# Two dense attention layers: blocks of 512 queries instead of 256, and the side that is held still in the value product exchanged

## The reference, cut to what matters

```python
h = maximum(layernorm(x), 0);  x = x + L0(h, adj)        # first block, not touched here
h = maximum(layernorm(x), 0);  x = x + L1(h, adj)        # two layers of this form:
def gat_layer(x, W, adj):                                # x 4096 x 256, adj 4096 x 4096
    Wh, Ws = split(x @ W, 2, axis=-1)
    a = softmax(Wh @ Ws.T, axis=-1) * adj
    return leaky_relu(a @ Wh + x, 0.01)
```

## Time and profile before

| | us |
|---|---|
| median of 3 runs | 2611.19 (2610.53 to 2612.25) |
| the profiled execution | 2612.48, its span from first to last instruction 2610.7 |
| first block | up to 925 |
| projection and attention of g0 | 925 to 981, 981 to 1770 |
| projection and attention of g1 | 1774 to 1817, 1817 to 2605 |

### The profile page before, as it was taken

How to read it: one execution, slowest core, us unless ns; L and a number is a source line. 1 busy time by engine, 2 the same in 40 slices (tenths; PEclk the granted TensorE clock), 3 DMA queues, 4 the chain that set the end, 5 groups by cost and what they waited for, 6 DMA issues and landing times. The chain is left out here.

```text
span 2610.7 us, 47736 instructions
## 1 busy us (share of the span) xinstructions
PE 2480.9 (95%) x18360; PEld 2346.5 (90%) x18360; DVE 2210.9 (85%) x2942; ACT 1694.8 (65%) x2348; POOL 1523.2 (58%) x932
## 2 busy tenths in 40 slices
PE   4699999999999979999999999987999999999997
PEld 2588888888888869999999999987999999999997
DVE  8899999998989646888888888894788888888888
ACT  6899999999999754555555555553555555555554
POOL 3899999999999802444434444350245445444446
PEclk8799999999999989999999999999999999999999
DMA  3332323233323021333333333233133333333333
GB/s 109 107 94 89 94 90 93 91 95 93 95 90 93 13 100 47 96 97 107 94 98 102 98 96 107 90 114 109 58 101 114 102 95 120 95 105 111 102 98 106
DMA packets 100980, 248.21 MB, mean 95 GB/s; under 512 B 9360, under 2 KB 51088, under 8 KB 100752
## 3 DMA queue, kind: packets, MB, share of 16 engines
q1 hardware_dynamic: 98880, 243.30, 30.5%
q10 hardware_dynamic: 1872, 1.84, 0.2%
HBM read 232.52 MB, written 12.58 MB: 94 GB/s over the span
## 5 line engine op out<-in xcount | busy, mean ns | idle before, releaser
L91 PE MATMUL l0b_acc<-l_h_parts,l0b_turned_hi 128*128 128x512 f32 x1984 | 727.2, 406 | 19.3 <-POOL l0b_turned_lo L541 19.2
L541 POOL TENSOR_TENSOR l0b_turned_lo<-l0b_turned,l0b_turned_hi 128x1024 fp32r<-128x1024 f32 x256 | 614.3, 2416 | 45.0 <-ACT l0b_turned_hi L578 43.3
L92 PE MATMUL l0b_acc<-l_h_parts,l0b_turned_lo 128*128 128x256 f32 x1984 | 558.3, 281 | 0.0
L1133 POOL TENSOR_TENSOR g0b_sum_wide<-g0b_sum_wide,g0b_slab 128x512 f32<-128x512 f32 x240 | 311.3, 1297 | 396.1 <-DVE g0b_masked_psum L1241 386.0
L1133 POOL TENSOR_TENSOR g1b_sum_wide<-g1b_sum_wide,g1b_slab 128x512 f32<-128x512 f32 x240 | 315.5, 1315 | 339.5 <-DVE g1b_masked_psum L1241 328.7
L91 PEld LDWEIGHTS l0b_acc<-l_h_parts,l0b_turned_hi 128*128 128x128 f32 x1984 | 376.0, 190 | 112.7 <-POOL l0b_turned_lo L541 29.7
L92 PEld LDWEIGHTS l0b_acc<-l_h_parts,l0b_turned_lo 128*128 128x128 f32 x1984 | 374.2, 189 | 0.8
L578 ACT CAST l0b_turned_hi<-l0b_turned 128x1024 fp32r<-128x1024 f32 x256 | 268.1, 1047 | 67.6 <-PE l0b_acc L92 50.1
L80 PE MATMUL g0b_acc<-g_wh_parts,g0b_part_hi 128*128 128x256 f32 x1024 | 293.6, 287 | 6.8 <-DVE g0b_part_lo L1247 5.7
L80 PE MATMUL g1b_acc<-g_wh_parts,g1b_part_hi 128*128 128x256 f32 x1024 | 293.6, 287 | 5.6 <-DVE g1b_part_lo L1247 4.5
L80 PE MATMUL g0b_score_psum<-g0b_q_block,g_vt_hi 128*128 128x256 f32 x1024 | 290.3, 284 | 2.5 <-DVE g0b_q_block L1277 1.4
(11 more groups left out here) (231 smaller groups left out, 7218.6 us busy)
## 6 DMA issues: line engine op xcount, KB each, us to landing
g_adj_ring<-in_adj_blocks_dram SPq DMA_DIRECT2D x256, 512.0 KB, 3.6
l_adj_ring<-in_adj_quads_dram SPq DMA_DIRECT2D x128, 512.0 KB, 3.5
l0b_x_in<-in_x_dram SPq DMA_DIRECT2D x32, 128.0 KB, 2.4
x_rows<-l0b_x SPq DMA_DIRECT2D x32, 128.0 KB, 2.4
g0a_rows<-x_rows SPq DMA_DIRECT2D x8, 512.0 KB, 5.8
g0b_y<-x_rows SPq DMA_DIRECT2D x16, 256.0 KB, 4.0
v_rows<-g0b_y SPq DMA_DIRECT2D x16, 256.0 KB, 4.5
g1a_rows<-v_rows SPq DMA_DIRECT2D x8, 512.0 KB, 5.8
```

Of the source, the lines that this page charges most:

```text
L91: pe.matmul(out, lhs_hi, rhs, start=first, stop=False)
L92: return pe.matmul(out[:, width:], lhs_lo, rhs[:, :width], start=False, stop=False)
L541: pool.tensor_tensor(turned_lo[:, m % PART_RING, :, :], turned[:, m % TURN_RING, :, :], turned_hi[:, m % PART_RING, :, :].bitcast(F32), AL ...
L1133: pool.tensor_tensor(sum_wide[:], sum_wide[:], half_of(c, e), ALU.add).then_inc(summed, 1)
```

## The change

A block has 512 queries (`BLOCK = BANK`), a chunk has 2 key tiles (`CHUNK = 2`), so a layer has 8 blocks of 16 chunks, and still 128 chunks with 1024 elements per partition each. `score` moves 512 columns of queries. In the value product the 128 columns of Wh are held still and 512 queries of the parts move, so that `acc` holds the output turned, and 12 matmuls make a chunk. `TO_SHIFT`, `TO_SPLIT`, `TO_WEIGH` follow PER and become 17, 18 and 19 steps. At a block's end ACT copies `acc` (`copy_out`), PE turns it back with 8 transposes (`turn_out`), DVE drains from there, ACT does the leak.

The high and low parts of Wh no longer fit: the projection stores them to memory, a quad of 1 MB at a time (`store_wh`), and waits for all of them at its end; the attention fetches 512 KB with every chunk (`fetch_wh`) once PE has done the chunk three before, and the adjacency behind it.

Three banks (`side_psum`) now serve every short-lived result of PE in turn: queries, scores, maximum, sum and the turned-back output. A product waits for whatever used its bank three turns before.

```diff
-    BLOCK = 256
+    BLOCK = BANK
-    CHUNK = 4
+    CHUNK = 2
-    SLOTS = 11
+    SLOTS = PER + 3
-        wh_parts = keep.sbuf("wh_parts", [P, T, 2, D], F32R)
...
+                    def store_wh(c):
+                        sp.wait_ge(out_lo_made, OUTS * (c + 1))
+                        wait(sp, wh_stored, 16 * c)
+                        stage = wh_stage[:, (c % 2) * OUTS:(c % 2 + 1) * OUTS, :, :, :].bitcast(F32)
+                        sp.dma_start(wh_dram[:, c, :], stage.rearrange("p o t h d -> p (o t h d)")
+                                     ).then_inc(wh_stored, 16)
...
+                    sp.wait_ge(wh_stored, 16 * QUADS)
...
                     def out_high(c):
+                        wait(act, wh_stored, 16 * (c - 1))
...
+            COPY_OUT, TURN_OUT, DRAIN = TURN_SUM + 1, TURN_SUM + 2, TURN_SUM + 3
...
+            def turns_of_step(n):
+                b = block_at(n, Q_AT)
+                if b is not None and b + 1 < BLOCKS:
+                    yield from (("query", KT * (b + 1) + m) for m in range(KT))
+                if n < CHUNKS:
+                    yield "score", CHUNK * n
+                b = block_at(n, TURN_OUT)
+                if b is not None:
+                    yield from (("out", 2 * b + k) for k in range(2))
+                for kind, offset in (("max", TURN_MAX), ("sum", TURN_SUM)):
+                    b = block_at(n, offset)
+                    if b is not None:
+                        yield kind, b
+                if n < CHUNKS:
+                    yield "score", CHUNK * n + 1
...
+                    def fetch_wh(c):
+                        wait(sp, products, c - ADJ_SLOTS + 1)
+                        sp.dma_start(wh_ring[:, c % ADJ_SLOTS, :, :, :].rearrange("p t h d -> p (t h d)").bitcast(F32),
+                                     wh_by_chunk[:, c % PER, :]).then_inc(chunk_in[c % ADJ_SLOTS], 16)
...
+                    def copy_out(b):
+                        act.wait_ge(products, PER * (b + 1))
+                        wait(act, out_turned, 2 * b)
+                        act.copy(turned_out[:], acc[:]).then_inc(out_copied, 1)
...
-                        for i in range(SUBS):
-                            cols = slice(i * P, (i + 1) * P)
+                        for d in range(KT):
+                            cols = slice(d * P, (d + 1) * P)
                             last = three_products(
-                                pe, acc[:, i, 0:D], (part_hi[:, c % 2, q, cols], part_lo[:, c % 2, q, cols]),
-                                (wh_parts[:, j, 0, :], wh_parts[:, j, 1, :]), j == 0, j == T - 1)
+                                pe, acc[:, d, :],
+                                (wh_ring[:, c % ADJ_SLOTS, e, 0, cols], wh_ring[:, c % ADJ_SLOTS, e, 1, cols]),
+                                (part_hi[:, c % 2, e, :], part_lo[:, c % 2, e, :]), j == 0, j == T - 1)
```

More of the change, by code:

```diff
@@ L1089, in block_at, with bank, tile_of @@
                 return b if rest == 0 and 0 <= b < BLOCKS else None
+            def turns_of_step(n):
[13 more added lines that the diff above has]
+                    yield "score", CHUNK * n + 1
+            order = [("query", m) for m in range(KT)] + [use for n in range(ENDS) for use in turns_of_step(n)]
+            turn_of = {use: turn for turn, use in enumerate(order)}
+            def bank(kind, k):
+                return side_psum[:, turn_of[kind, k] % BANKS, :]
+            def tile_of(c, e):
+                return slab[:, c % SLOTS, e, :]
             with nc.Block() as block:
@@ L1170, in q_high @@
                     def q_high(b):
-                        act.wait_ge(q_made, b + 1)
-                        wait(act, score_made, HALVES * (b - 1))
-                        act.copy(q_block[:, b % 2, 0, :, :], q_bank(b)).then_inc(q_hi_made, 1)
+                        for m in range(KT):
+                            act.wait_ge(q_made, KT * b + m + 1)
+                            if m == 0:
+                                wait(act, score_made, CHUNK * PER * (b - 1))
+                            act.copy(q_block[:, b % 2, 0, m, :], bank("query", KT * b + m)).then_inc(q_hi_made, 1)
                     def normalise(b):
@@ L1304, in _, with wait_for_bank @@
                             totals(b)
-                        if drained is not None:
-                            leak(drained)
+                        if n < CHUNKS:
+                            join_max(n, 0)
                 @block.tensor
                 def _(pe):
-                    def wait_for_bank(turn):
-                        before = turn - SCORE_BANKS
-                        if before in half_at:
-                            pe.wait_ge(score_taken, half_at[before] + 1)
-                        if before in q_at:
-                            pe.wait_ge(q_lo_made, q_at[before] + 1)
+                    def wait_for_bank(kind, k):
+                        turn = turn_of[kind, k]
+                        if turn < BANKS:
+                            return
+                        last_kind, j = order[turn - BANKS]
+                        if last_kind == "score":
+                            pe.wait_ge(score_taken, j + 1)
+                        elif last_kind == "query":
+                            pe.wait_ge(q_lo_made, j + 1)
+                        elif last_kind == "max":
+                            pe.wait_ge(neg_step, 3 * j + 1)
+                        elif last_kind == "sum":
+                            pe.wait_ge(total_step, 2 * j + 1)
+                        else:
+                            pe.wait_ge(scaled, 2 * (j + 1))
@@ L1366, in turn_sum, with turn_out @@
                                                 ident)
                         last.then_inc(sum_turned, 1)
-                    def weigh(c, q):
+                    def turn_out(b):
+                        pe.wait_ge(out_copied, b + 1)
+                        for k in range(2):
+                            wait_for_bank("out", 2 * b + k)
+                            for i in range(SUBS // 2):
+                                here = slice((k * SUBS // 2 + i) * P, (k * SUBS // 2 + i + 1) * P)
+                                for d in range(KT):
+                                    last = pe.transpose(bank("out", 2 * b + k)[:, i * D + d * P:i * D + (d + 1) * P],
+                                                        turned_out[:, d, here], ident)
+                            last.then_inc(out_turned, 1)
```

296 lines of the change are left out of this document (148 added, 148 removed).

## The result

The kernel after takes **2740.78 us** (median of 4 runs, 2732.89 to 2745.62) beside 2611.7 us before: ratio 1.0492, 95% interval 1.0475 to 1.0509. It is slower, by 129 us where 109 were forecast. Its profiled execution took 2741.81 us, its span 2740.0.

What follows compares the result with a forecast made beforehand. PE was taken to bound the steady attention. Attention +33.1 us a layer, twice +66, projections +33 and ends +10 made +109 us, 2720 us on the median; range 2640 to 2765 us.

Steps and rivals of the forecast that it cites:

- What one product costs: PE's products: one 512 wide takes 235 ns where two 256 wide take 240; each ns is worth 5.9 us.
- The bounds: Limits for one 512-wide product on PE: 227 ns if overhead is paid once per product, 240 if it goes with columns.
- the first rival: PE's products: overhead goes with each product, 227 ns wide, −48 us, giving 2672 us; chance 0.19.
- The steady steps: Attention outside the tail: −14.7 us a layer, step 5.64 us, PE stays the bound, adjacency lands after 5.4 us without delaying PE.
- the forecast's own first two waits: Block end, step 36: PE loses 0.75 us at the output's turning back and 0.75 us at the second score.
- A bank is waited for at each block's end: Shared banks at six block ends: PE loses 4.7 us each, 3.2 of it behind DVE's drain; +28.2 us a layer.
- The clock "at full": Sign of being right: PE halts of about 3 us, six a layer, leave the granted clock at full.
- The third rival: Step 37's halt lowers the clock, 2.4 us more for each of 12, or a transfer is late: 2749 us; chance 0.16 together with 240 ns pace.
- A longer tail: Attention's tail: value products lag 19 steps, not 11; a fetch loop makes it 80 us, 75 without; net +11.9 us.
- Between the phases, and the ends: Projections +33 us from storing Wh at 5.2 us a store; last outputs and g1's residual sum, ends +10 us.
- the signs that the forecast listed as wrong: Pace under 217 ns, stores under 4 us, no PE wait on the drain, or PE waiting every step for the parts.
- steps 36 and 37: Steps at a block's end where bank order was followed: PE loses 0.75 and 0.75 us, then 3.2 us.

Runs made afterwards that it cites:

- the pace measurement: Separate kernel computing none of the reference: sequences of 97 products, wide, narrow and alternating, alone or beside other engines; 226.6 ns wide, 120 ns narrow.
- the first edit: The kernel after with a block's drain one step earlier on DVE, behind that step's last maximum; 2669.34 us, ratio to before 1.0218.
- the cure: The kernel after with the adjacency fetched two chunks ahead, once VectorE frees its slot, on its own semaphores; 2668.6 us, ratio to before 1.0219.
- the last kernel: Earlier drain, early adjacency, overlapping stores, staging tile kept into attention, and first three adjacency fetches moved behind the barrier; 2587.06 us, ratio to before 0.9906.
- the kernel with both cures: The kernel after with the drain one step earlier and the adjacency fetched two chunks ahead; 2611.78 us, ratio to before 0.9999.
- each half: The kernel after with only the drain one step earlier (2669.34 us), or only the adjacency fetched two chunks ahead (2668.6 us).

## Why the prediction was right, and where it was not

The time, 2741, lies in the range and 21 us over the forecast. But one of the forecast's steps was 49 us too dear, and two others, the late transfers (some 30 us beyond what it had) and the clock (some 20), were together about as much too cheap.

- **What one product costs.** This term was mis-sized: 235 ns taken, 226.7 measured. 8.3 ns x 5880 products are 49 us that the kernel got back. The bounds held the value, and the reason for the lower one (the 13.3 ns are paid once a product) is what the pace measurement showed. The doubt written beside it ("its neighbours are narrow ones") was the cause, and the first rival, 227 ns, had this term right.
- **The steady steps.** "A landing up to 3 us later still costs nothing" failed. The landing was sized well (5.25 for 5.4), but the argument followed only the parts to PE's value products. ScalarE's high part stands ahead of its copies of the scores, and those free PE's banks; the forecast saw this at a block's end and took it for nothing in the steps of the queries and the maximum. By the two kernels: 653.1 us with halts and the adjacency ahead, 678.6 with it late, so 25.5 us in g0 and 24.3 in g1. 1.65 us at each of the six block ends are the forecast's own first two waits (it had 1.5); the other 15 or so a layer it had at nothing. In g0 those are 7.6 us of idle time in the steps named and 8.4 us of longer busy time, 5 of them by more half clock (27.3 for 17.1 us); the last 3 stay open, and so does where g1, with 17.1 us of half clock in both kernels, has its 5.
- **A bank is waited for at each block's end.** Right: 3.20 us, six a layer, released by VectorE's drain, and 4.85 us a block end for 4.7.
- **The clock "at full"** failed. It was forecast from a fall 4.1 us after the end of work, and 3.20 us of idle time brought it down in ten of twelve cases. The third rival had the mechanism at 29 us; 44.4 us at half clock are 22, and the first edit gave back 20.5.
- **A longer tail.** The loop over the fetch is there, and the cure gives the 75 us that the forecast named without it, nearly (79.2 and 76.3). Its size was low: 84.9 and 91.1 for 80, 16 us in all. In g1's tail the clock fell as well, mean 0.90.
- **Between the phases, and the ends.** Right in mechanism and size: +28.0 for +33, and +8.6 for +10. The restart at half clock came, 10.2 us at 1.2 GHz in each layer; where it didn't (the last kernel), g0's stage up to the first weighing was 2.5 us shorter than in after.

So for the stretch from first weighing to last score of g0: 624.6 us if nothing waits (the kernel with both cures). By the forecast's terms it would be 8.3 ns x 2813 = 23 us more for the slower pace and 28 for the block ends, 676. Measured are 678.6: late transfers and the clock took the place of the 23. The right total is partly luck. None of the signs that the forecast listed as wrong appeared, since they were set for larger errors (a pace under 217 ns, PE waiting in every step). The walk of the banks, with the transfer's landing in it, was the right tool; it was done for steps 36 and 37 alone, and should have been done for every step in which something beside the scores takes a bank.

## What to carry to other kernels

Wider products pay their fixed 13 ns once, so the change is worth its gain where PE sets the time, but a step with other lengths reaches its buffers at other times: walk each bank and each ring slot back to its last user with the new step time before trusting that the lead is still there. An operation that frees a bank must not stand, in its engine's order, behind something that waits for the present step; here one drain moved by a few lines was worth 71 us. When several small stalls stand in one stream, cure them together before judging the change: each half left the kernel 2.2% slower than before, both made it level, and with the passage from projection to attention mended it was 0.9% faster.

## What the runs showed of the hardware

- A product of these operands (float32 in the rows, written as fp32r) costs its columns at 2.4 GHz and some 13.3 ns at 512 and at 256 columns; alternating the two widths costs 6.4 ns a pair more. The other engines' work changes it by nothing that shows (353.1 ns a pair with and without it).
- An idle PE of 3.20 us brought the granted clock to 0.50 in ten of twelve cases; 2.39 and 2.14 us ahead of the attentions did not. In the tails, where PE waits in nearly every step, the clock fell around a wait of 2.26 us (1821.8 in after). What tells the two spared halts from the ten stays open.
- A store of 1 MB needs 4.9 to 5.0 us to land; with two under way the projection still shortened by 3.8 and 6.5 us.
- Three DMA issues in a row held SyncE for 2.41 us, and through the barrier every other engine.
